# A fused GroupNorm, attention and projection kernel: equal units of half a projection, transposes in the ring of the score banks

## What is computed

```python
xn = silu(group_norm(x, gn_scale, gn_offset))          # 32 groups of 16 channels
q, k, v = split(xn @ w_qkv, 3)                          # 8 heads of 64 channels
sim = (q * 64 ** -0.5) @ k.T                            # per head, 1024 x 1024
out = softmax(sim) @ v
out = out @ w_out + b_out + x
```

## Time and profile before

| | |
|---|---|
| median of 3 runs | 4330.39 us |
| the profiled execution | 4330.27 us |
| its span, first to last instruction | 4328.5 us |
| PE busy | 3827.5 us (88%) |
| DVE busy | 3022.1 us (70%) |
| ACT busy | 2851.5 us (66%) |
| POOL busy | 1717.7 us (40%) |
| mean granted clock of PE | 0.958 |
| DMA | 211.25 MB, 49 GB/s |

### The profile page before, as it was taken

How to read it: one execution, slowest core, us unless ns; L and a number is a source line. 1 busy time by engine, 2 the same in 40 slices (tenths; PEclk the granted TensorE clock), 3 DMA queues, 4 the chain that set the end, 5 groups by cost and what they waited for, 6 DMA issues and landing times.

```text
span 4328.5 us, 90413 instructions
## 1 busy us (share of the span) xinstructions
PE 3827.5 (88%) x32844; PEld 2133.3 (49%) x32844; DVE 3022.1 (70%) x3936; ACT 2851.5 (66%) x3202; POOL 1717.7 (40%) x1226
## 2 busy tenths in 40 slices
PE   3889999898998989989899998989989899898997
PEld 1445545454554545545455454545545455454553
DVE  5676676867767676676766768677676766767664
ACT  2676676767767676676766767667676766766664
POOL 1243443433434343343434434334343333434333
PEclk8989999999999999999999999999999999999999
DMA  2111112122021121212111121220311212121111
GB/s 75 37 38 47 57 30 74 31 59 60 16 82 36 50 55 32 73 30 59 45 47 57 30 74 31 59 59 16 82 37 50 55 31 74 30 59 45 40 54 36
DMA packets 105031, 211.25 MB, mean 49 GB/s; under 512 B 13392, under 2 KB 13392, under 8 KB 104656
## 3 DMA queue, kind: packets, MB, share of 16 engines
q1 hardware_dynamic: 104656, 205.84, 17.8%
HBM read 71.57 MB, written 33.55 MB: 24 GB/s over the span
## 4 chain that ended last, share of the span: by engine, by line
PE 52%; DVE 19%; issue 16%; ACT 4%; POOL 4%; SPq 2%; DMA 2%; DVEq 1%; POOLq 0%; ACTq 0%
PE SD L891 27%; PE PV L1004 9%; DVE Pl L760 5%; DVE mx L707 5%; PE TP L905 5%; PE ST L971 4%; PE ST L970 4%; POOL Pl L460 3%; SPq L353 2%; DVE work L750 2%; ACT QK L521 2%; DMA work<-in_x 1%; PE TP L912 1%; ACT Ph L562 1%; PE SD L947 1%
## 5 line engine op out<-in xcount | busy, mean ns | idle before, releaser
L559 ACT ACTIVATE P<-ST,cns 128x1024 f32<-128x1024 f32 x1024 | 1142.0, 1115 | 753.6 <-PE ST L971 536.3
L460 POOL TENSOR_TENSOR Pl<-P,Ph 128x1024 f16<-128x1024 f32 x512 | 1212.0, 2367 | 920.4 <-ACT Ph L562 917.3
L707 DVE TENSOR_REDUCE mx<-TP 128x1 f32<-128x1024 f32 x1024 | 1248.3, 1219 | 234.0 <-PE TP L905 223.8
L562 ACT ACTIVATE Ph<-ST,cns 128x1024 f16<-128x1024 f32 x1024 | 1134.8, 1108 | 0.0
L1004 PE MATMUL PV<-V,Ph 128*128 128x129 f16 (+2 forms) x10240 | 893.7, 213 | 133.9 <-DVE Pl L760 122.8
L1004 PEld LDWEIGHTS PV<-V,Ph 128*128 128x128 f16 x10240 | 790.6, 99 | 385.0 <-DVE Pl L760 150.7
L1004 PE MATMUL PV<-V,Pl 128*128 128x65 f16 x8192 | 861.9, 195 | 0.0
L970 PE MATMUL ST<-QK 128*128 128x512 f16 x2048 | 807.3, 394 | 0.4
L971 PE MATMUL ST<-QK 128*128 128x512 f16 x2048 | 807.1, 394 | 0.0
L1004 PEld LDWEIGHTS PV<-V,Pl 128*128 128x128 f16 x8192 | 740.1, 100 | 89.7 <-issue 17.1
L905 PE MATMUL TP<-QK 128*128 128x512 f16 x2048 | 640.6, 396 | 105.4 <-DVE QK L711 53.8
(11 more groups left out here) (91 smaller groups left out, 2889.6 us busy)
## 6 DMA issues: line engine op xcount, KB each, us to landing
QK<-QK SPq DMA_DIRECT2D x384, 256.0 KB, 4.8
work<-in_x SPq DMA_DIRECT2D x128, 256.0 KB, 2.8
res<-in_x SPq DMA_DIRECT2D x128, 256.0 KB, 2.8
out<-res SPq DMA_DIRECT2D x128, 256.0 KB, 2.0
V<-in_L_conv_w_qkv SPq DMA_DIRECT2D x1, 3072.0 KB, 10.4
P<-in_L_conv_w_out SPq DMA_DIRECT2D x1, 1024.0 KB, 12.3
bias<-in_L_conv_b_out SPq DMA_DIRECT2D x1, 256.0 KB, 7.4
gam<-in_L_conv_gn_scale SPq DMA_DIRECT2D x1, 2.0 KB, 12.0
```

The source lines that it names most:

```text
L460: nc.gpsimd.tensor_tensor(Pl[:, v % 4, :], P32[:, v % 2, :], Ph[:, v % 4, :], ALU.subtract).then_inc(lo_pool, 1)
L559: nc.scalar.activation(P32[:, v % 2, :], ST[:, v % 2, :], ACT.Exp, scale=cns[:, 0:1])
L562: nc.scalar.activation(Ph[:, v % 4, :], ST[:, v % 2, :], ACT.Exp, scale=cns[:, 0:1]).then_inc(exp_done, 1)
L707: nc.vector.reduce_max(mx[:, hh, qb:qb + 1], TP[:], AX.X).then_inc(top_drained, 1)
```

## The change

- **Every unit carries half a projection.** JOBS replaces SIDE: each pair of units (even u, then odd) has one projection, its first 6 matmuls in the even unit and its last 6 in the odd one. Steps 0 and 1 have 4 qk and 4 out, steps 2 and 3 have 4 qk and 4 v. The last image has no v and no qk for a pair after it.
- **Transposes leave SD.** They take a turn in the two score halves of ST (TURNS): 8 transposes at once, 4 turns for x (xt) and 4 for the output (ot) per image, each drained by ACT with one copy of 1024 columns; DVE subtracts 1024 columns for ot. `wait_ring` waits for the entry two places back in that ring. "mean" and "var" go to TP.
- **PE's order**: even unit: scores, turn, V, maximum, first half; odd unit: scores, turn, maximum, second half, V, shift. `times_v` waits separately for the two low halves.
- **Pl is split by columns**: in every unit DVE writes its first 512 and POOL its last 512. P32 and Ph of a unit wait for both.
- **Buffers**: X has two places by turns of images; the normalised form xn is written over x in its own place, z has storage of its own, the loads of x have theirs. The loop body covers two images, 7 times round instead of 14. x comes in 4 loads of 512 KB.
- **The copy of V** is a DMA issued by SP at (0, 4) instead of an instruction of DVE.
- Statistics, coefficients, silu and bias additions are spread over other units (BN_AT to LATE_BIAS_AT); the first turns of the next image's x are in step 0 instead of step 1.

The number of matmuls, exponentials, maxima and projections is the same. The core of the diff:

```diff
-SIDE = [
-    {0: "qk", 1: ("ot", 2, 0), 2: "qk", 3: ("ot", 2, 1), 4: "qk", 5: "qk", 6: ("ot", 3, 0),
-     7: ("ot", 3, 1), 8: "out", 10: "out", 12: "out", 13: "out", 14: "out", 15: "out"},
-    {0: "qk", 1: "xt", 2: "qk", 3: "xt", 4: "qk", 5: "xt", 6: "qk", 7: "xt", 8: "xt", 9: "xt", 10: "xt",
-     11: "xt", 13: "out", 14: "out"},
-    {0: ("ot", 0, 0), 1: ("ot", 0, 1), 2: "mean", 3: "qk", 4: "var", 5: "qk", 6: "qk", 7: "qk", 12: "v",
-     13: "v", 14: "v"},
-    {0: "qk", 1: ("ot", 1, 0), 2: "qk", 3: ("ot", 1, 1), 4: "qk", 5: "qk", 8: "v", 10: "v", 12: "v",
-     13: "v", 14: "v"},
...
+JOBS = [["qk"] * 4 + ["out"] * 4, ["qk"] * 4 + ["out"] * 4, ["qk"] * 4 + ["v"] * 4, ["qk"] * 4 + ["v"] * 4]
+def unit_job(step, u, first=False, last=False):
+    j = u // 2
+    kind = JOBS[step][j]
+    if kind == "qk":
+        return [] if last and step == 3 else [("qk", (step + 1) % 4, "qk"[j % 2], j // 2)]
+    if kind == "out":
+        return [] if first else [("out", j - 4 + 4 * step)]
+    return [] if last else [("v", j - 4 + 4 * (step - 2))]
...
+TURNS = {(0, 1): ("xt", 0), (0, 3): ("xt", 1), (0, 4): ("ot", 3), (0, 7): ("xt", 2), (0, 9): ("xt", 3),
+         (2, 0): ("ot", 0), (2, 8): ("ot", 1), (3, 4): ("ot", 2)}
...
+def ring_of(first=False, last=False):
+    ring = []
+    for v in range(UNITS):
+        ring += [("score", v)] + unit_turn(v // 16, v % 16, first, last)
+    return ring
...
+BN_AT = {(0, 5): (0, 2), (0, 7): (4, 6), (0, 11): (1, 3), (0, 13): (5, 7)}
+AGGREGATE_AT, NEWTON_AT, COEF_AT = (0, 14), (1, 5), (1, 7)
+Z_AT = [(1, 8), (1, 11), (1, 13), (2, 1), (2, 4), (2, 7), (2, 11), (2, 13)]
+TANH_AT = [(1, 9), (1, 12), (1, 15), (2, 3), (2, 5), (2, 9), (2, 12), (2, 15)]
+SILU_AT = [(1, 11), (1, 13), (2, 0), (2, 4), (2, 7), (2, 11), (2, 13), (3, 0)]
+LOW_XN_AT = [(1, 12), (1, 14), (2, 1), (2, 5), (2, 8), (2, 12), (2, 14), (3, 1)]
+BIAS_AT = {(3, 0): 0, (3, 2): 1, (3, 5): 2, (3, 6): 3}
+LATE_BIAS_AT = {(1, 0): 4, (1, 2): 5, (1, 6): 6, (1, 8): 7}
...
+        X = sb("X", [P, 2, CC, TOK], F32)
+        xn = X[:, :, :, :].rearrange("p a c n -> p (a c n)").bitcast(F16).rearrange(
+            "p (a c h j n) -> p a c h j n", a=2, c=CC, h=2, j=2)
+        x_in = sb("x_in", [P, 2, CH], F32)
+        z = sb("z", [P, 2, HALF], F32)
+        th = sb("th", [P, 2, HALF], F32)
...
+            def load_x(image, i):
+                src = x_blocks[bass.ds(sp.snap(image * TB + 2 * i), 2)].rearrange("o p c -> p o c")
+                wait(sp, xt_filled, 4 * image + i)
+                sp.dma_start(x_in[:], src).then_inc(x_loaded[i], 16)
...
+            def move_v(b):
+                sp.wait_ge(pv_done, UNITS * b + 1)
+                sp.dma_start(V[:, :, 0:4, :], V[:, :, 8:12, :]).then_inc(v_moved, 16)
...
-                nc.gpsimd.tensor_tensor(Pl[:, v % 4, :], P32[:, v % 2, :], Ph[:, v % 4, :], ALU.subtract
+                nc.gpsimd.tensor_tensor(Pl[:, v % 4, HALF:], P32[:, v % 2, HALF:], Ph[:, v % 4, HALF:], ALU.subtract
...
+            def step(b, s, par, cnt, first=False, last=False):
                 for u in range(16):
                     v = 16 * s + u
+                    if v % 4 == 2 and not (first and v == 2):
                         sums_out(b, v // 4 - 1)
+                    for use in job_before(s, u, first, last):
+                        side(use, image_of(use, b, s), cnt)
+                    exponentials(b, v, cnt)
+                    for use in unit_turn(s, u, first, last):
+                        turned(use, image_of(use, b, s), 1 - par, cnt)
+                    if (s, u) in TANH_AT and not last:
+                        silu_tanh(b + 1, 1 - par, TANH_AT.index((s, u)))
+                    if (s, u) in Z_AT and not last:
+                        silu_z(b + 1, 1 - par, Z_AT.index((s, u)))
...
+            def low_output(pair, image, slot):
+                dve.wait_ge(ot_filled, 4 * image + pair + 1)
+                dve.wait_ge(ot_hi, 4 * image + pair + 1)
+                nc.vector.tensor_tensor(OT[:, 1, pair, :], ST[:, slot], OT[:, 0, pair, :], ALU.subtract
+                                        ).then_inc(ot_lo, 1)
...
+            def step(b, s, par, cnt, first=False, last=False):
+                turned = []
                 for u in range(16):
                     v = 16 * s + u
+                    if (s, u) == AGGREGATE_AT and not last:
+                        dve.wait_ge(bn_done, b + 2)
+                    for use in (shift_before(s, u, last) if not (first and v == 0) else []):
+                        top_use(use, b + 1, cnt)
+                    for use in job_before(s, u, first, last):
+                        side(use, image_of(use, b, s), cnt)
+                    for use, slot in turned:
+                        low_output(use[1], image_of(use, b, s), slot)
+                    if not (first and v == 0):
+                        low_probs(b, v - 1)
+                    if v % 4 == 3 and not (first and v == 3):
+                        sums(b, v // 4 - 1)
                     for use in unit_max(s, u, last):
+                        top_use(use, b + 1, cnt)
+                    cnt.next_slot()
+                    turned = [(use, cnt.next_slot()) for use in unit_turn(s, u, first, last)]
...
+                for c, i, j in PASSES if part is None else PASSES[:6] if part == 0 else PASSES[6:]:
...
+            def turn(use, image, slot, blocks):
+                if use[0] == "xt":
+                    pe.wait_ge(x_loaded[use[1]], 16 * (image + 1))
+                    for t in range(2):
+                        for c in range(CC):
+                            ins = nc.tensor.transpose(ST[:, slot, bass.ts(2 * c + t, P)],
+                                                      blocks[:, t, bass.ts(c, P)], ident32[:])
+                    ins.then_inc(xt_filled, 1)
+                else:
+                    pe.wait_ge(o_normed, 16 * image + 4 * (use[1] + 1))
+                    for t in range(TB):
+                        ins = nc.tensor.transpose(ST[:, slot, bass.ts(t, P)], O32[:, use[1] % 2, t, :], ident32[:])
+                    ins.then_inc(ot_filled, 1)
...
+            def wait_ring(entry, b, first, last):
+                ring = ring_of(first, last)
+                at = ring.index(entry)
+                if at < 2:
+                    wait(pe, exp_done, UNITS * b - 1 + at)
+                    return
+                kind, n = ring[at - 2]
+                if kind == "score":
+                    pe.wait_ge(exp_done, UNITS * b + n + 1)
+                elif kind == "xt":
+                    pe.wait_ge(xt_out, 4 * (b + 1) + n + 1)
+                else:
+                    pe.wait_ge(ot_lo, 4 * (b - 1 if n == 3 else b) + n + 1)
...
+            def times_v(b, v, cnt):
...
+                for i in range(2):
+                    pe.wait_ge(lo_pool if i else lo_dve, UNITS * b + v + 1)
...
+            def step(b, s, par, cnt, first=False, last=False):
                 for u in range(16):
                     v = 16 * s + u
                     before = (b, v - 2) if v >= 2 else (b - 1, UNITS + v - 2)
+                    wait_ring(("score", v), b, first, last)
+                    scores(b, v, cnt.next_slot(), cnt)
+                    for use in unit_turn(s, u, first, last):
+                        wait_ring(use, b, first, last)
+                        turn(use, image_of(use, b, s), cnt.next_slot(), x_in)
+                    if u % 2 == 0:
+                        if not (first and v < 2):
+                            times_v(*before, cnt)
+                        for use in unit_max(s, u, last):
+                            top_use(use, image_of_tops(b, s, u), cnt)
+                        for use in unit_job(s, u, first, last):
+                            side(use, image_of(use, b, s), par_of(use, s, par), cnt, part=0)
+                    else:
+                        for use in unit_max(s, u, last):
+                            top_use(use, image_of_tops(b, s, u), cnt)
+                        for use in unit_job(s, u, first, last):
+                            side(use, image_of(use, b, s), par_of(use, s, par), cnt, part=1)
+                        if not (first and v < 2):
+                            times_v(*before, cnt)
+                        for use in unit_shift(s, u, last):
+                            top_use(use, b, cnt)
+                        for use in unit_stats(s, u, last):
+                            top_use(use, b + 1, cnt)
```

## The result

| | before | after |
|---|---|---|
| median | 4330.25 us (4 runs) | 3914.7 us (4 runs, 3912.08 to 3916.27) |
| ratio, 95% interval | | 0.904 (0.9025 to 0.9056) |
| the profiled execution, its span | 4330.27, 4328.5 us | 3913.47, 3911.7 us |
| mean granted clock | 0.958 | 0.989 |
| first image between marks | 250.9 us | 228.4 us |

A forecast was written before the change was run, and what follows sets the result against it. TensorE bounds the kernel, busy 88%, its gaps coming from placement of work. Per image 222 of matmuls + 4.4 waits + 3.6 restarts = 230 us; with start, first image, 14 images and end, 3810 us; range 3710 to 3970.

The forecast's parts named there:

- Floor, 222: TensorE's matmul work in one image where nothing holds it: 222 us of the 262.9 measured before.
- Steps (1) and (2): Half a projection per unit, 3.29 us of TensorE work each, and a new order in pairs; the 7.3 us low-half waits go.
- Clock: TensorE's low-clock stretches, about 10 us per image, go together with the gaps.
- rival C: One late landing per step leaves TensorE standing 2 to 3 us and its clock falls: 240 per image, 3965 us; chance 0.11.
- Step (4), V: Copy of V by DMA from SP: 3.17 us of DVE and a 2.84 us gap go; landing in 4 to 12 us.
- (5), x and placement: x loaded one turn ahead, not behind placement's copies: TensorE's wait of up to 5 us goes; placement slack 0.9.
- (6), turns in the ring: Transposes 8 at a time in the score ring: ACT copy 1.1 to 1.2 us, DVE subtraction about 1.3, hidden but for (2,1).
- D: Added waits within V and projections each expose a weight load, 64 x 0.18: 238 per image, 3935 us; chance 0.10.
- A: POOL's lock holds DVE in every unit, making DVE the bound: 254 per image, 4180 us; chance 0.12.
- B: As A, with DVE also idle 0.7 per pair for ACT's copy: 276 per image, 4520 us; chance 0.04.
- (7), waits 4.4 and restarts 3.6: Normalisation spread: late coefficients and silu make TensorE wait, all waits summing to 4.4 us; V's restarts add 3.6 per image.
- (3): Low halves split over DVE (0.68 us) and POOL (1.15); POOL's lock costs DVE 29 us per image, not the path.

## Why the prediction was right, and where its size was off

The time lies in the range; of the band of the forecast itself, 224 to 236 us per image and 3715 to 3905 in all, the image is inside with 235.4 and the time 10 us outside. The sum as written gives 3811.2, not 3810. It was cut at the start of unit (0, 7) of the first and of the last image, and there the timelines of TensorE (first matmul of L1051 in that unit: 155.2, 384.0 and 3683.4) show where the 102 us of the span lie:

- *Up to unit (0, 7).* 155.2 against 154: +1.2.
- *First image.* 384.0 - 155.2 = 228.8 against 218: +10.8. Of these 5.7 are the error per image; the other 5 are that I took over 12 us as the worth of the missing output projections from the earlier trace rows. In after they are worth 7: TensorE waits 17.2 us for maxima and ms in this image, where the later ones have 5.5.
- *14 images.* 3299.4, or 235.7 each, against 230: +79. (The marks give 235.4, as the last of them goes out earlier in its image than the others, with no load of x ahead of it.)
- *Behind it.* 3911.7 - 3683.4 = 228.3 against 217.4: +10.9. The rest of step 0 (30.1), step 1 (53.6) and half of step 2 (27.8) came within 0.1 us of what I gave or below it, the epilogue 39.8, given 38.9. The 24 units without a projection took 77.0 with the last V, given 65.9: the starts of their scores are 3.09 us apart on average, where I took the earlier trace rows with 2.65. The chain there (3839 to 3851) runs through DVE: maximum, an ms of 1.35, low halves of 0.82 and 1.01; and the granted clock was 0.91 from 3810 to 3850, 3.6 us of it.

**Per image, step by step.** *Floor, 222*: right; without POOL's half the image takes 225.8. *Steps (1) and (2), halves even the units*: right. A pair takes 6.63 and no low half is waited for. *Clock*: right, 1.00; rival C with its 240 is wrong. *Step (4), V, and (5), x and placement*: right. V's 1040 KB land in 6.4 us (5.4 to 7.8), x's 512 KB in 3.8, and PE waits 0.4 us for the placement in the whole run. *(6), turns in the ring*: right; ACT's copy took 1.02 and DVE's subtraction 1.21, given 1.1 to 1.2 and 1.3. *D*, exposed weight loads: wrong; V's 18 take 0.71 in the chain. *A and B*: DVE did not become the bound; its busy time came out at 207.6 against the given 209, 180.0 without POOL's half against the given 180. That the first fits is luck in part: its low halves lost 17 us an image (64 times 956 - 691 ns), not 29, and the other 10.6 are in operations for which I had charged little or nothing. *(7), waits 4.4 and restarts 3.6*: the waits were 9.2; 235.4 - 222 - 9.2 = 4.2 are left, which holds the restarts and whatever the floor lacks.

**The step that was mis-sized is (3), with the sum of (7).** I had the mechanism. But I charged POOL's hold to DVE's low half and called it time "of DVE, not of the path"; beside it I allowed a hold for one operation of the coefficients, and perhaps for silu behind an odd unit's maximum, hidden. ms I took at the length that it has alone, 0.23. (The 0.92 per pair in that step doesn't follow from its own 4.95 and 4.1 either, which make 0.85, or 27 us instead of 29.) The hold also takes ms (0.99 at 2146.55), z (1.37), the sums (1.23), and these stand on or before the path: 5.5 of waits for ms instead of 2.4. I listed (2, 0), (2, 4), (3, 0) as the late places and those were late (1.25, 1.40 and 1.46 of wait, given 1.0, 0.7, 0.7), as was (1, 8) behind the coefficients (1.83, given 1.3 to 1.5); (2, 9) with 1.04, where the subtraction of a turned output comes before the maximum and ms falls on a POOL start, I did not list. The earlier trace rows shows exactly this, four columns that take as long as POOL's instruction, and I did not carry it over to the other small operation, ms.

What stays open: how the 9.6 divide. Of the 5.5 us of waits for ms the rows give 2.7 to ms itself and the rest to late maxima; how much of the lateness is the hold and how much DVE's order, they don't say. The run with ms on POOL took the hold from ms, but put a second operation in its place.

## What to carry to other kernels

Before work goes to POOL, list DVE's instructions with two inputs in SBUF, and its tensor_scalar operations and casts from SBUF to SBUF, tiny ones first, and find the one whose result TensorE waits for: its worst case is its own length plus that of one POOL instruction. The length of a single POOL instruction sets this price; how often it is paid follows from the order of both engines and from POOL's total time. If POOL must run beside them, try its instruction cut in two; here it paid even at 1.3 to 1.7 times POOL's time. Evening out the work between units can pay even where no engine is at its limit: whole projections cost 13 us an image in one order and 26 in the other.

## What was unexpected of the hardware

- Twice the columns in half as many POOL instructions is much worse: ms, 128 x 4, took 1.07 us on average with 1024 columns at once (2.14 us), 0.45 with 512 (1.21 us), 0.24 with one column.
- Among DVE operations from SBUF to SBUF some are held by POOL and some are not: a reciprocal took 0.17 us and bn_stats 0.68 with POOL in the middle of its 2.13 us, a sum of 128 x 192 waited it out (2.17 us).
- Cutting 512 columns into four of 128 takes POOL 501 ns each, 2.0 us in sum against 1.22, and yet frees DVE (846 against 946 ns).
- DVE operations whose source is in PSUM, maximum and subtraction of a projection, keep their 1.22 and 0.75 us in all of these kernels.
- A copy of 1040 KB within SBUF by DMA landed in 5.4 to 7.8 us beside running engines, with no effect on TensorE that can be seen.
